# Graph network kernel: 16 ranked stretches of 15 groups, ten gathered groups per stretch, and indirect clearing of padding rows

## The reference

```python
# first network; n1 = src, n2 = dst, mlp = leaky_relu between two products
future = mlp(concat(x[n2], edge_attr))   # 96 -> 128 -> 64
future_agg = segment_sum(future, n1)
past = mlp(concat(x[n1], edge_attr))
past_agg = segment_sum(past, n2) / max(counts, 1)
x = layernorm(x + mlp(concat(past_agg, future_agg)) + x)
# second network: this layer twice, then layernorm(x + h)
agg = segment_sum(h[src], dst) * deg_inv
h = agg @ Wl.T + bl + h @ Wr.T
h = relu(h / max(norm(h), 1e-12))
```

## Time and profile before

| what | value |
|---|---|
| median of 3 runs | 7910.08 us (7909.2 to 7927.37) |
| the profiled execution, its own time | 7941.06 us |
| the profiled execution, its span | 7939.0 us |
| mean granted clock of TensorE over the span, as a share of full speed | 0.770 |

### The profile page before, as it was taken

One profiled execution on the slowest core, in us unless ns is written; L12 is line 12 of the kernel. 1 busy time (PEld: TensorE's weight loads), 2 busy tenths in 40 slices (PEclk: granted clock), 3 DMA queues, 4 the chain that ended last, 5 costly groups with the idle time before them and its releaser, 6 DMA issues. The chain is left out here.

```text
span 7939.0 us, 139237 instructions
## 1 busy us (share of the span) xinstructions
PE 6681.0 (84%) x39214; PEld 5228.7 (66%) x39430; DVE 4236.9 (53%) x16294; ACT 2139.5 (27%) x4708; POOL 6022.3 (76%) x4866
## 2 busy tenths in 40 slices
PE   5889988899988998989889888796888876888883
PEld 4778877778777777878777777664444444444442
DVE  5777777777777743333333333334555554555553
ACT  2222222222222222222222222243333324333333
POOL 5888888888888888888888888734777775777783
PEclk7777777776777766676676667667999996999995
DMA  4333333333333332222222222232222223222221
GB/s 129 34 34 34 34 35 34 34 34 34 34 34 34 34 29 27 27 28 27 27 27 27 27 27 27 28 93 71 66 64 66 65 55 78 65 64 65 65 62 51
DMA packets 710748, 363.73 MB, mean 46 GB/s; under 512 B 552256, under 2 KB 658148, under 8 KB 710194
## 3 DMA queue, kind: packets, MB, share of 16 engines
q0 software_dynamic: 325280, 163.91, 20.1%
q1 hardware_dynamic: 382948, 195.00, 10.1%
q10 hardware_dynamic: 2286, 1.95, 0.1%
HBM read 279.51 MB, written 80.96 MB: 45 GB/s over the span
## 5 line engine op out<-in xcount | busy, mean ns | idle before, releaser
L664 POOL DMA_INDIRECT future<-sbuf,sidx x1564 | 2489.2, 1592 | 484.3 <-issue 457.0
L650 POOL DMA_INDIRECT gbuf<-in_x_dram,gidx x1564 | 1592.2, 1018 | 481.5 <-issue 472.2
L1537 PE MATMUL bank<-at_dst,rows 128*128 128x512 bf16 x2744 | 1084.8, 395 | 15.0 <-issue 3.3
L1389 POOL DMA_INDIRECT gb<-x,nidx x728 | 855.3, 1175 | 283.3 <-issue 168.0
L1389 POOL DMA_INDIRECT gb<-h,nidx x728 | 862.4, 1185 | 262.1 <-issue 170.1
L1502 ACT CAST rows<-bank 128x384 bf16<-128x384 f32 x1372 | 657.2, 479 | 1497.7 <-PE bank L1521 1497.0
L1535 PE MATMUL bank<-at_dst,rows 128*128 128x512 bf16 x2528 | 1002.8, 397 | 0.0
L976 PEld LDWEIGHTS bank<-w1pe,featT 96*128 96x128 f32 x3128 | 723.3, 269 | 306.1 <-issue 305.6
L1427 DVE TENSOR_SCALAR at_dst<-iota,metaf 128x512 bf16<-128x512 f16 x2744 | 827.3, 352 | 7.3 <-PE bank L1537 5.3
L977 PE MATMUL bank<-w1px,srcT 65*128 65x128 f32 x3128 | 816.5, 354 | 0.0
L976 PE MATMUL bank<-w1pe,featT 96*128 96x128 f32 x3128 | 816.4, 354 | 0.0
(11 more groups left out here) (260 smaller groups left out, 11464.5 us busy)
## 6 DMA issues: line engine op xcount, KB each, us to landing
laneb<-lanes SPq DMA_DIRECT2D x392, 224.0 KB
gbuf<-in_x_dram,gidx POOLq DMA_INDIRECT x1564
comb<-in_edge_attr_dram SPq DMA_DIRECT2D x391, 64.0 KB
future<-sbuf,sidx POOLq DMA_INDIRECT x1564, 3.2
blkb<-blkrow SPq DMA_DIRECT2D x210, 98.0 KB
future<-zero POOLq DMA_DIRECT2D x16, 800.0 KB, 17.8
fut<-future SPq DMA_DIRECT2D x100, 125.0 KB
gb<-x,nidx POOLq DMA_INDIRECT x732, 2.6
```

What stands on the lines that cost most here:

```text
L650: pool.indirect_dma_start(out=gbuf[:, b, q, :], out_offset=None, in_=x[:, :], in_offset=bass.IndirectOffsetOnAxis(ap=gidx[:, b, q:q + 1], ...
L664: pool.indirect_dma_start(out=future[q][:, :], out_offset=bass.IndirectOffsetOnAxis(ap=sidx[:, b, q:q + 1], axis=0), in_=sbuf[:, b, q, :], ...
L1389: pool.indirect_dma_start(out=gb1[:, m, q, :], out_offset=None, in_=frm[:, :], in_offset=bass.IndirectOffsetOnAxis(ap=nidx[:, i % 2, m, q: ...
L1537: pe.matmul(psL[i % 2][:, :], rows16[:, j % AR, t % 2, 2 * D:4 * D], at_dst[:, t % DR, :], start=(b == 0), stop=(b == BLOCKS - 1)).then_in ...
```

## The change

The number of stretches goes from 14 to 16 and the gathered groups of a stretch from 13 to 10. So 240 groups are ranked instead of 210, and 160 entries per layer (151 real groups and 9 padding entries) are gathered instead of 182 (181 real ones and 1 padding entry). `TAKE` becomes 5, 14, 24, 33, 43, 52, 62, 71, 81, 90. The tables `x1` and `h1` get 128 padding rows instead of 44; these are cleared by two indirect transfers with the indices N to N + 127 in place of two direct ones. The temporary `placed` goes, and `ranked` is overwritten in place.

```diff
@@ -38,11 +38,11 @@
 SBG = 15
-SBS = 14
+SBS = 16
 PEG = SBG * SBS
-POOLG = 13
+POOLG = 10
@@ -80,8 +80,8 @@
-    x1 = nc.dram_tensor("x1", [NP, D], F32).ap()
-    h1 = nc.dram_tensor("h1", [NP, D], F32).ap()
+    x1 = nc.dram_tensor("x1", [N + P, D], F32).ap()
+    h1 = nc.dram_tensor("h1", [N + P, D], F32).ap()
@@ -307,8 +307,10 @@
                 pool.dma_start(xT[:, N:NW], zero[0:D, 0:W]).then_inc(sA_pad, 16)
-                pool.dma_start(x1[N:NP, :], zero[0:NP - N, 0:D]).then_inc(sA_pad, 16)
-                pool.dma_start(h1[N:NP, :], zero[0:NP - N, 0:D]).then_inc(sA_pad, 16)
+                pool.wait_ge(s_iota, 6)
+                for t in (x1, h1):
+                    pool.indirect_dma_start(out=t[:, :], out_offset=bass.IndirectOffsetOnAxis(ap=dump_i[:, 0:1], axis=0),
+                                            in_=zero[:, 0:D], in_offset=None).then_inc(sA_pad, 16)
@@ -1025,7 +1027,6 @@
-        placed = tmp("placed", [P, PEG, TILES])
@@ -1090,11 +1091,11 @@
-                dve.scalar_tensor_tensor(out=placed[:, :, :], in0=keys[:, :, 0, :], scalar=float(P), in1=ranked[:, :, :],
+                dve.scalar_tensor_tensor(out=ranked[:, :, :], in0=keys[:, :, 0, :], scalar=float(P), in1=ranked[:, :, :],
...
-                dve.scalar_tensor_tensor(out=rel[:, 0:PEG, :], in0=placed[:, :, :], scalar=-1.0e6, in1=rel[:, 0:PEG, :],
+                dve.scalar_tensor_tensor(out=rel[:, 0:PEG, :], in0=ranked[:, :, :], scalar=-1.0e6, in1=rel[:, 0:PEG, :],
@@ -1292,9 +1293,9 @@
-        ONE_SLOT = [0, 1, 2, 3] * 3 + [2]
-        SUM_SLOT = [0, 1] * 6 + [0]
-        TAKE = [15 * m // 2 + 5 for m in range(POOLG)]
+        ONE_SLOT = [0, 1, 2, 3] * 2 + [0, 1]
+        SUM_SLOT = [0, 1] * 5
+        TAKE = [19 * m // 2 + 5 for m in range(POOLG)]
@@ -1353,7 +1354,7 @@
-            blocks_of = frm.rearrange("(b p) d -> p b d", p=P)
+            blocks_of = frm[0:NP, :].rearrange("(b p) d -> p b d", p=P)
```

## The result

The changed kernel takes **7808.1 us** (median of 4 runs, 7803.06 to 7815.2) against 7909.64 us of the kernel before (4 runs beside it, 7908.77 to 7927.37): a ratio of **0.9867 (0.985 to 0.9884)**, 101.5 us less. It is faster, as forecast, by 1.3%, inside the range, and by about half of the 189 us that the sum gave.

A forecast was written before the change was run, and what follows sets the result against it. GpSimd's gathers, never stopping, were taken to bound the layers. Layers -202 us, edge stage +12 and node stage +1 gave -189, so 7721 us against the median of 7910.08; stated range 7640 to 7835.

The forecast's parts named there:

- the 189 us that the sum gave: Whole kernel: two layers -202 us, edge stage +12, node stage +1, together -189 us.
- TensorE's floor: Layers: TensorE's work for 98 steps and 10 `sums` at full clock, 57.6 us a stretch.
- I cost them at nothing: Layers: the pacing gates of GpSimd's gathers would be open in time and add 0 us.
- the 60.5 us a stretch: Layers: forecast stretch, between GpSimd's 59.4 and TensorE's 61.1 us, with 58 and 64 as ends.
- the forecast's own range: Whole kernel: 7686 to 7773 us, from stretches of 59.4 to 62.1 us; the forecast has 59%.
- the second rival: Layers: gathers lengthen by half, giving 64.0 us a stretch and 7833 us in all; chance 14%.
- The proportional lengthening: Layers: more `at_dst` per gathered group raise 0.91 us to 1.18, a stretch to 62.1, making -202 into -150.
- the signs that the prediction named: Layers: gather starts over 960 to 1000 us, mean near 1.18, TensorE's gather waits well below 198.6, clock 0.95 or above.
- 0.91 us per group: Layers: time a group of four gathers loses beside runs of `at_dst`, within GpSimd's 5.94 us per group.
- part of the gain goes back: Layers: lengthening grows to 1.37 us per group, -45 us per layer, 7833 us in all; chance 14%.
- The slower rival: Layers: VectorE's runs shut GpSimd out, lengthening 1.82 us per group, 7977 us; slower from 1.61 on; chance 9%.
- Half of the low-clock time: Layers: TensorE at 1.2 GHz loses 49 us a layer, 3.5 us per stretch; if kept, it needs 61.1.

The follow-up runs named there:

- e9_before_ahead12: Kernel before, with gather gates opened 12 steps ahead instead of 4 and over the stretch's border: 7911.32 us, 1.0008.
- e7_before_dr11: Kernel before, with only VectorE's lead over TensorE cut from 14 steps to 11: 7733.71 us, 0.9761.
- e1_gate: Changed kernel, with gather gates cut at zero over the whole layer and no longer within each stretch: 7779.72 us, 0.9845.
- e2_ahead12: Changed kernel, with gates reaching over the stretch's border and opened 12 steps ahead instead of 4: 7701.54 us, 0.9748.
- e11_before_dr12: Kernel before, with only VectorE's lead over TensorE cut from 14 steps to 12: 7807.61 us in a single execution.
- e4_dr11: Changed kernel, with gates 12 steps ahead over the stretch's border and VectorE's lead cut from 14 to 11: 7658.24 us, 0.9689.
- e3_pad: Changed kernel, with padding entries reading 128 different cleared rows instead of row 0 128 times: 7810.34 us, 0.9883.
- e8_best: Changed kernel, with gates 12 steps ahead over the border, VectorE's lead at 11 and padding entries reading 128 different rows: 7639.13 us, 0.9645.
- e6_clear_only: Kernel before, with only the larger padded tables, cleared by two indirect transfers: 7928.52 us, 1.0005.

## Why the prediction was right, and where its sum was not

**Right: what bounds a layer, and that it moves.** GpSimd was full, and three groups fewer per stretch shortened it; e9_before_ahead12 and e7_before_dr11 show both halves of "full": earlier gates bring nothing, shorter gathers bring nearly all that they save. TensorE's floor was worked out as 57.6 us and measured as 57.53.

**The step of the working that failed: "So the gates of the next group are open while TensorE still works on this one, and I cost them at nothing."** They cost 65 and 59 us of GpSimd's time per layer. The working held each gate against VectorE's place in `add_sums`, where VectorE stands longest, within one stretch and for the last gather of a group. It left out what happens between stretches. Ten groups have 40 gathers on 98 steps, so gates are 2.45 steps apart, but the last one of a stretch is at step 92 and the first of the next, cut at zero, at the count that stands for step 99: seven steps (from 93 to 99, six, in the kernel before). A GpSimd that needs its whole stretch is behind its gates and sees nothing of this, and that was so before. With slack it arrives early, waits there, and begins the next stretch late by what it waited. e1_gate shows that the cut is a part of it, e2_ahead12 that the pacing as a whole is worth some 107 us. So the 60.5 us a stretch became 61.7 and 62.7, and two layers gave -151 in the profiles instead of -202; without the idle time GpSimd's stretch would be 58.3 and 59.7, close to its forecast 59.4. With gates that do cost nothing the layers take 978.7 + 951.6 = 1930 us, 237 less than before.

**Where luck helped.** 7808 lies outside the forecast's own range, 7686 to 7773. It is inside the stated one because that was stretched to the second rival's 7835, and that rival's cause, a lengthening grown by half, did not come about. The proportional lengthening that the working set against itself (1.18 us per group) gave -150 for the layers, and the profiles gave -151; that too agrees by chance, as the lengthening did not grow at all. None of the signs that the prediction named was GpSimd's idle time itself; the starts of the gathers, over 1005.5 us in the second layer, fell just outside their 960 to 1000.

**The lengthening of gathers was sized right.** The prediction kept 0.91 us per group; 4 x (1.147 - 0.952) = 0.78 and 4 x (1.177 - 0.952) = 0.90 were measured. The rival "part of the gain goes back" needed 1.37 and gives 7833; the time went towards its figure by another way. The slower rival needed 1.61, and nothing came near it. What it said of the place is true all the same: the lead decides how long the gathers are. In the trace of before, 602 of the 1456 gathers have no `at_dst` beside them and take 0.952 us on average; the 487 that meet a run of three or more (each begun at most 0.30 us after the one before it) take 1.59. That is what the row of the 2.03 us gather showed, and in the changed kernel it is the same. A gather of GpSimd, and VectorE in order of time beside it:

```profile
5787.69 1.72 POOL L1390 DMA_INDIRECT gb<-x,nidx  x1 [0.30 <-issue]
```

```profile
5787.76 0.21 DVE L1446 TENSOR_TENSOR acc<-acc,bank 64x64 f32 x1 [1.20 <-PE bank L1548]
5787.90 1.39 DVE L1428 TENSOR_SCALAR at_dst<-iota,metaf 128x512 bf16<-128x512 f16 x5
```

The Trainium skill (SBUF — State Buffer, "Who interferes with whom") says that VectorE in a two-port mode, which `tensor_scalar` can enter, and GpSimd exclude each other: whichever issues first holds the shared port pair for the whole instruction, and the other is blocked. The runs agree in the direction: shorter leads, shorter gathers. They don't bear out that any meeting costs a wait, since 211 gathers of before that meet single `at_dst` only take 0.99 us on average. No run here shows which mode `at_dst` runs in, so that the ports are the cause is argued and not shown; that the lead is, e7_before_dr11 and e11_before_dr12 show.

**The clock.** Half of the low-clock time was to stay (3.5 us a stretch at TensorE). It did not: 0.99 in both layers, and 1.00 in the second layer of e4_dr11, where TensorE hardly waits. As the waits went, the time at 1.2 GHz went with them. This weighs little here, since TensorE alone did not set the pace of the changed kernel, but with the kept low clock e4_dr11 would, by the prediction's own working, have stood at 61.1 and not 57.53.

**The last stretch: +12 per layer forecast (0 to 22).** 70.9 and 70.4 us, with the last pair 71.9 and 71.4, against 61.74 and 62.71 make +10 and +9. The reason was right: in e3_pad and e8_best distinct rows take the lengthening away. The time that the packets of GpSimd's queue (q0) took, as a share of the 16 DMA engines, stands last, after packets and megabytes; the last stretch of the first layer, first in the changed kernel (6411 to 6479), then in e3_pad (6420 to 6482):

```profile
q0 software_dynamic: 1184, 1.21, 71.0%
```

```profile
q0 software_dynamic: 1198, 1.23, 6.9%
```

The median from issue to landing of these 36 gathers is 5.4 us in the one and 2.4 in the other.

**The edge stage: +12 forecast (8 to 16), +22 between the two profiles.** Over all traces of this study it lasts 4998 to 5016 us with 14 stretches (five traces) and 5013 to 5032 with 16 (eight), in the middle some +17. A ranked group takes 13.06 us against 12.67 of an unranked one in the changed kernel, as forecast, so the 30 groups are worth +12; the other 5 us are no more than traces of one kernel differ by among themselves, and stay open. The line that was cut into windows before, now 934:

```profile
126.00:2826.00 2700.00, 175.90 (x824) 0.73 0.31 34
3300.00:5100.00 1800.00, 121.59 (x567) 0.69 0.28 27
```

824 / 4 = 206 groups in 2700 us are 13.1 us a group, and 567 / 4 = 142 in 1800 are 12.7.

**The clearing** took 1.06 + 0.96 us, the low end of 2.0 to 3.2, and is hidden, as e6_clear_only shows. **The end** (from the last `rows_of` on) is 9 us shorter between the two profiles; traces with 16 stretches lie at 176 to 179 us, those with 14 at 180 to 185. The prediction had no term for it, and its cause was not tried.

**The base.** The sum was made against a profile 31 us above the median and taken over to the median unchanged. The 138 us between the two profiles would have to be set beside the -189, and the 101.5 of the medians beside what the forecast makes of an average run. Nearly all of the 31 us lie in the layers. The profile of e9_before_ahead12, whose edit made no difference, is at the median (7913.27 us): its edge stage takes 5002.8 us, as before, but its layers 1075.3 and 1063.6, 28 us less than those of before. Held against it, the change gave -123 in the layers and not -151, +21 in the edge stage and -5 at the end, together -107, near the 101.5 of the medians. Two layers of 980 us would there be -179, and the sum an estimated 7744 us. This rests on one trace as the average run.

## What to carry to other kernels

When work is taken off a full engine, work out again every gate that it used to reach late: those that never held it can be the next bound, as here, and the border between two rounds of a loop is a place where a gate formula can jump. The engine that a wait names need not be where the remedy is: here GpSimd's gathers got shorter when VectorE was kept from running far ahead, and that one number was worth more than the rearrangement. And compare medians with medians: the trace of before, 31 us above its median, made the gain look a third larger.

## What was not expected of the hardware

- GpSimd's time to write out one gather depends on how VectorE's work is bunched, also where its amount is the same: with 98 `at_dst` and 52 gathers per stretch each time, the mean went from 1.18 to 1.09 to 1.03 us as the lead went from 14 to 12 to 11.
- A gather that reads one row 128 times is slower than one that reads 128 rows. In the two lines of q0 above, the packets took 71.0% of 68 us and 6.9% of 62 us for the same 1.2 MB, some eleven times as long (an estimate from these). e8_best, with distinct rows in the padding, takes 9 to 10 us less in the last stretch than e4_dr11, over 36 such gathers. TensorE in the last stretch of the first layer of the changed kernel:

```profile
6463.66 0.74 PE L1548 MATMUL bank<-oneh,gb 128*64 128x64 f32 x8 [2.80 <-DMA gb<-x,nidx]
```

It waits 2.80 us for a transfer, where it waited 0.86 for the one padding group of before.
